# A mixture-of-experts drain of 34 slots instead of 36: five slots hold four experts of 32 tokens each

## The reference

```python
x = x + xattn(layernorm(x), ctx, ctx, Wq, bq, Wk, bk, Wv, bv, Wd, bd)
def ffn(h, w_red, wg, W1, b1, W2, b2):          # h: 4096 x 256, from layernorm(x)
    logits = (h @ w_red) @ (wg / norm(wg)).T    # 8 experts
    gates = softmax(logits); score = max(gates); idx = argmax(gates)
    u = gelu(h @ W1[idx] + b1[idx])             # 256 -> 512, own expert only
    return (u @ W2[idx] + b2[idx]) * score      # 512 -> 256
x = x + ffn(layernorm(x), ...)
```

## Time and profile before

| | |
|---|---|
| median of 3 runs | 344.08 us (343.32 to 344.24) |
| the profiled execution | 343.6 us |
| its span in the trace | 341.8 us |
| PE busy | 322.5 us, 94% of the span |
| DVE, POOL, ACT busy | 74%, 70%, 58% |
| TensorE clock granted | full in every slice |
| DMA | busy 0.9 and more until 190 us, then about 0.25 |

### The profile page before, as it was taken

How to read it: one execution, slowest core, us unless ns; L and a number is a source line. 1 busy time by engine, 2 the same in 40 slices (tenths; PEclk the granted TensorE clock), 3 DMA queues, 4 the chain that set the end, 5 groups by cost and what they waited for, 6 DMA issues and landing times.

```text
span 341.8 us, 10746 instructions
## 1 busy us (share of the span) xinstructions
PE 322.5 (94%) x3723; PEld 270.3 (79%) x3723; DVE 252.6 (74%) x718; ACT 199.7 (58%) x532; POOL 238.9 (70%) x379
## 2 busy tenths in 40 slices
PE   6999899999999999999788799989999999999995
PEld 5777678888888888777666688979898999996485
DVE  7545698888898888899887756885866666665563
ACT  1001577787778777867874745784567533443451
POOL 3598699999989999978888767552765545554323
PEclk9999999999999999999999999999999999999999
DMA  6699899999999999999999112240222222222100
GB/s 231 223 287 303 244 265 255 257 271 251 260 276 288 308 312 315 305 293 286 308 349 396 48 33 79 70 139 33 78 82 77 63 75 66 73 66 78 33 15 32
DMA packets 54838, 63.45 MB, mean 186 GB/s; under 512 B 36335, under 2 KB 45696, under 8 KB 54785
## 3 DMA queue, kind: packets, MB, share of 16 engines
q1 hardware_dynamic: 50544, 52.77, 52.7%
q0 software_dynamic: 3456, 9.12, 9.1%
q10 hardware_dynamic: 784, 0.87, 0.7%
HBM read 41.59 MB, written 21.68 MB: 185 GB/s over the span
## 4 chain that ended last, share of the span: by engine, by line
PE 77%; DVE 8%; issue 5%; ACT 4%; POOL 3%; DMA 2%; DVEq 1%; ACTq 0%; SPq 0%; POOLq 0%
PE bQ L1357 15%; PE bL L1307 7%; PE bKV L1118 7%; PE bY L1172 7%; PE bQ L1214 7%; PE bKV L1307 7%; PE bKV L1115 7%; PE bO L1138 5%; PE bL L1127 4%; PE bA L1226 3%; PE bT L1319 2%; DMA r<-in_xc 2%; PE bQ L1350 2%; PE bKV L1295 1%; PE bO L1273 1%
## 5 line engine op out<-in xcount | busy, mean ns | idle before, releaser
L1357 PE MATMUL bQ<-w,wA 128*128 x256 | 61.1, 381 | 1.5 <-issue 1.1
L418 POOL TENSOR_TENSOR x<-ql,mask 128x1024 f32<-128x1024 f32 x32 | 60.6, 1893 | 2.7 <-DVE r L748 0.5
L1000 ACT ACTIVATE pad<-ql 64x512 f32<-64x512 f32 x64 | 40.0, 625 | 22.2 <-DMA ql<-qkv_scr 21.8
L1357 PEld LDWEIGHTS bQ<-w,wA 128*128 128x128 f32 x256 | 46.2, 190 | 8.2 <-issue 3.2
L480 POOL DMA_INDIRECT out<-r,ids x23 | 23.2, 1010 | 41.3 <-DVE r L910 41.3
L500 POOL DMA_INDIRECT r<-row_scr,idg x36 | 37.2, 1033 | 14.7 <-issue 14.7
L1023 ACT ACTIVATE ax<-bA,mask 128x256 f32<-128x256 f32 x91 | 36.3, 473 | 3.5 <-PE bA L1226 3.3
L1172 PE MATMUL bY<-wD,oT 128*128 128x265 f32 x128 | 34.6, 392 | 1.4 <-ACT oT L988 1.3
L1078 ACT ACTIVATE wA<-bL,r 128x128 f32<-128x128 f32 x68 | 19.4, 373 | 25.3 <-PE bL L1307 25.3
L1214 PE MATMUL bQ<-wA,r 128*128 128x265 f32 x128 | 33.9, 387 | 0.3 <-DVE wA L536 0.3
L1115 PE MATMUL bKV<-wA,r 128*128 128x256 f32 x128 | 33.0, 380 | 1.1 <-DMA r<-in_xc 0.6
(11 more groups left out here) (213 smaller groups left out, 688.4 us busy)
## 6 DMA issues: line engine op xcount, KB each, us to landing
qkv_scr<-qkv SPq DMA_DIRECT2D x16, 768.0 KB, 4.7
ql<-qkv_scr SPq DMA_DIRECT2D x32, 384.0 KB, 5.8
r<-in_xc SPq DMA_DIRECT2D x15, 512.0 KB, 5.8
row_scr<-cat SPq DMA_DIRECT2D x32, 133.5 KB, 6.1
w1b<-in_W1b SPq DMA_DIRECT2D x8, 514.0 KB, 7.1
w<-in_W SPq DMA_DIRECT2D x8, 512.0 KB, 7.0
xt<-in_x SPq DMA_DIRECT2D x15, 256.0 KB, 5.9
b2b<-in_b SPq DMA_DIRECT2D x2, 512.0 KB, 6.8
```

The costliest lines, as they stand in the source:

```text
L418: eng.tensor_tensor(quarter(kx[:, z % 2, :]), spread(ql[z // 2 % 2][:, :, z % 2, 0:HD]), mask_k, ALU.mult).then_inc(S["kx"], 1)
L1000: i_ = eng.activation(pad[n, z % 3, :].rearrange("p (k g h d) -> p k g h d", k=2, g=NG_, h=2) [:, :, :, h, :], ql[z // 2 % 2][n, :, z % 2, ...
L1357: i_ = eng.matmul(down_bank(b)[:, 0:C], hT[b % 2][:, k, :], w2[:, bass.ds(eb * (KH * C) + k * C, C)], start=(k == 0), stop=(k == KH - 1))
```

## The change

- `NS` goes from 36 to 34. An expert's rest is put either into a whole slot or into quarters of 32 tokens; five slots hold four quarters each, of any four experts. They are no longer neighbours: `MIX_SLOTS` = (20, 23, 26, 29, 32). `S2` is 21.
- Which experts' rests get a whole slot goes by their size: `vector_late` ranks the eight rests (parts 1 to 3), and part 13 is shorter.
- A mixed slot's first and second product run as four tiles of 32 columns. The first expert's matrices are those in SBUF; the other three experts' are loaded again from DRAM by SP, in `sync_quarters` (six transfers of 512 KB for each mixed slot, in two sets of buffers that the attention stage leaves free; the third set waits for the first to be used).
- Both biases of a mixed slot are gathered by token from a new input `b12` (b1 and b2 of each expert in one row of 3 KB): `pool_bias`, one for each of steps 15 to 19. DVE adds the first as it copies the hidden values out; the gelu is one instruction over 512 columns instead of eight; the second bias takes one DVE instruction instead of two.
- `scalar_second` is gone.

The diff, cut:

```diff
-MIX = 3
-NS = NT + NE - 1 - MIX
+MIX = 5
+QUARTER = P // 4
+QUARTERS = P // QUARTER
+NS = ((NTOK + NE * (QUARTER - 1)) // QUARTER + QUARTERS - 1) // QUARTERS
...
-MIX_AT = NS - 3 - MIX
+MIX_STEP = 3
+MIX_SLOTS = tuple(NS - 2 - MIX_STEP * (MIX - 1 - j) for j in range(MIX))
...
+        def sync_quarters(eng, j):
+            if j == 0:
+                eng.wait_ge(S["texp"], 1)
+                eng.wait_ge(S["idg"], 1)
...
+            if j > 1:
+                eng.wait_ge(S["up"], MIX_SLOTS[j - 2] + 1)
+            e = [eng.value_load(texp[0:1, u:u + 1], min_val=0, max_val=NE - 1) for u in units(MIX_SLOTS[j])[1:]]
+            for h, e_h in enumerate(e):
+                eng.dma_start(first[j % 2][h], W1b.rearrange("e p n -> (e p) n")[bass.ds(e_h * P, P), 0:KC * HID]
+                              ).then_inc(S[f"first{j % 2}"], 16)
+            if j > 1:
+                eng.wait_ge(S["down"], MIX_SLOTS[j - 2] + 1)
+            for h, e_h in enumerate(e):
+                eng.dma_start(second[j % 2][h], W2.rearrange("e p n -> (e p) n")[bass.ds(e_h * P, P), :]
+                              ).then_inc(S[f"second{j % 2}"], 16)
...
+            if 0 <= s - BIAS_AT < MIX:
+                pool_bias(eng, s - BIAS_AT)
...
             if part == 2:
-                after(eng.scalar_tensor_tensor(odd, til, float(P), rest, ALU.mult, ALU.is_lt))
+                after(eng.scalar_tensor_tensor(key8, io_e[:, 0, :], 1.0 / 16, rem, ALU.mult, ALU.add))
+                after(eng.tensor_tensor(gt8, key8.unsqueeze(1).broadcast_to((P, NE, NE)),
+                                        key8.unsqueeze(2).broadcast_to((P, NE, NE)), ALU.is_gt))
+                eng.tensor_reduce(ftot, full_l, AX, ALU.add)
+                after(eng.tensor_reduce(rank, gt8, AX, ALU.add))
+                eng.tensor_scalar(q32, rem, (QUARTER - 1.0) / 2, ROUND_QUARTER, ALU.add, ALU.add)
+                after(eng.scalar_tensor_tensor(reach, rank, float(P), ftot.broadcast_to((P, NE)), ALU.mult, ALU.add))
+                eng.tensor_scalar(q32, q32, ROUND_QUARTER, None, ALU.subtract)
+                after(eng.tensor_scalar(w128, reach, float(WHOLE * P), float(P), ALU.is_lt, ALU.mult))
...
@@ vector_hidden
-                eng.tensor_copy(w1s[a % 2][:, 0:HID], bH[a % 2][:, :]).then_inc(S["hid"], 1)
+                eng.wait_ge(S[f"bias{j}"], 16)
+                eng.tensor_tensor(w1s[a % 2][:, 0:HID], bH[a % 2][:, :], bias[j][:, 0:HID],
+                                  ALU.add).then_inc(S["hid"], 1)
...
@@ tensor_up
-                        eng.matmul(bH[a % 2][0:HALF, :], gT[a % 2][:, c, 0:HALF],
+                        eng.matmul(bH[a % 2][0:QUARTER, :], gT[a % 2][:, c, 0:QUARTER],
                                    w1f[:, bass.ds(e0 * W1W + c * HID, HID)], start=(c == 0), stop=(c == KC - 1))
-                        i_ = eng.matmul(bH[a % 2][HALF:P, :], gT[a % 2][:, c, HALF:P],
-                                        second1[j][:, c * HID:(c + 1) * HID], start=(c == 0), stop=(c == KC - 1))
+                        for h in range(1, QUARTERS):
+                            i_ = eng.matmul(bH[a % 2][quarter_rows(h), :], gT[a % 2][:, c, quarter_rows(h)],
+                                            first[j % 2][h - 1][:, n], start=(c == 0), stop=(c == KC - 1))
```

More of the change, by code:

```diff
@@ L60 @@
 FILLS_ROWS = 8
-SECOND_AT = NEXT + 6
+BIAS_AT = NEXT + 7
 INVERSE_IN = (NEXT + 3, NEXT + 4)
@@ L97, in mixed, with quarter_rows, build @@
 def mixed(s):
-    return MIX_AT <= s < MIX_AT + MIX
+    return s in MIX_SLOTS
 def column(s):
-    return s if s < MIX_AT else s + NS - MIX_AT - MIX if mixed(s) else s - MIX
+    return NS - MIX + MIX_SLOTS.index(s) if mixed(s) else s - sum(1 for m in MIX_SLOTS if m < s)
 def units(s):
-    return [S1 + WHOLE + 2 * (s - MIX_AT) + h for h in range(2)] if mixed(s) else [column(s)]
-def build(nc, x, xc, wkvT, wqT, wdT, Wd, bkvq, bd, bd_col, w_redT, wgT_in, wg, W1b, W2, b2, out):
+    return [S1 + WHOLE + QUARTERS * MIX_SLOTS.index(s) + h for h in range(QUARTERS)]
+def quarter_rows(h):
+    return slice(QUARTER * h, QUARTER * (h + 1))
+def build(nc, x, xc, wkvT, wqT, wdT, Wd, bkvq, bd, bd_col, w_redT, wgT_in, wg, W1b, W2, b2, b12, out):
     f32, bf16, i32 = mybir.dt.float32, mybir.dt.bfloat16, mybir.dt.int32
@@ L203, in build @@
         ids = sb("ids", [P, NSP], i32)
-        texp = sb("texp", [P, S1 + UNITS], i32)
+        texp = sb("texp", [P, S1 + UNITS + MIX], i32)
         ohe = oh[:, :, :].rearrange("p n e -> p e n")
@@ L232, in build @@
         key, top, inc = late(0, NT - R1, NE), late(96, NT - R1), late(128, NE, NT)
-        rest, texc, shift, over, rank, delta, unit = (late(640 + 8 * k, NE) for k in range(7))
+        rest, texc, shift, full_l, rem, q32, key8, rank, reach, w128, uexc, delta = (late(384 + 8 * k, NE)
+                                                                                     for k in range(12))
+        ftot = late(480, 1)
+        gt8 = late(512, NE, NE)
         both, inc2 = late(2240, 2 * NE), late(2256, 2 * NE)
-        til, odd, tinc, oinc = both[:, 0:NE], both[:, NE:2 * NE], inc2[:, 0:NE], inc2[:, NE:2 * NE]
-        last8, far = late(2272, NE), late(2280, R1)
+        whole, part_q, tinc, uinc = both[:, 0:NE], both[:, NE:2 * NE], inc2[:, 0:NE], inc2[:, NE:2 * NE]
+        far = late(2280, R1)
         exc, slot, lim = late(704, NE, NT), late(960, NE, NT), late(1216, NE, NT)
@@ L252, in build @@
         bH = [bKV, bL]
-        second1 = [x0[:, W1W * j:W1W * (j + 1)] for j in range(MIX)]
-        first_bias = [x0[:, W1W * MIX + KH * j:W1W * MIX + KH * (j + 1)] for j in range(MIX)]
-        second2 = [fl(xt)[:, KH * C * j:KH * C * (j + 1)] for j in range(MIX)]
+        bias = [x1[:, (HID + C) * j:(HID + C) * (j + 1)] for j in range(MIX - 1)] + [sb("bias4", [P, HID + C])[:, :]]
+        B = KC * HID
+        taken_x0 = [x0[:, B * k:B * (k + 1)] for k in range(4)]
+        taken_xt = [fl(xt)[:, B * k:B * (k + 1)] for k in range(3)]
+        taken_q = [b[:, :, :, :].rearrange("p x t w -> p (x t w)")[:, 0:B] for b in (*qkv, *ql)]
+        first = [taken_xt, taken_x0[0:3]]
+        second = [[taken_x0[3], *taken_q[0:2]], [*taken_q[2:4], ax[:, :]]]
         def spread(in_):
@@ new lines, in vector_late @@
+                eng.tensor_scalar(q32, q32, ROUND_QUARTER, None, ALU.subtract)
+                after(eng.tensor_scalar(w128, reach, float(WHOLE * P), float(P), ALU.is_lt, ALU.mult))
+            if part == 3:
+                eng.tensor_tensor(whole, full_l, w128, ALU.add)
+                after(eng.scalar_tensor_tensor(part_q, w128, 0.0, q32, ALU.is_equal, ALU.mult))
+                after(eng.tensor_tensor_scan(inc2, one8[:, :], both, 0.0, ALU.mult, ALU.add))
+                after(eng.tensor_tensor(texc, tinc, whole, ALU.subtract))
+                eng.tensor_tensor(uexc, uinc, part_q, ALU.subtract)
+                after(eng.tensor_tensor(shift, texc, taken[:, :], ALU.subtract))
@@ L797, in vector_late @@
-                after(eng.tensor_scalar(delta, rank, -float(HALF), float(S2 * P), ALU.mult, ALU.add))
+                after(eng.tensor_tensor(lim, tinc.unsqueeze(2).broadcast_to((P, NE, NT)), slot, ALU.is_le))
             if part == 5:
@@ L862, in vector_weights @@
                 eng.wait_ge(S["texp"], 1)
-            if slotted(n):
-                held_v[n] = [eng.value_load(texp[0:1, u:u + 1], min_val=0, max_val=NE - 1) for u in units(n)]
-                if mixed(n) or n in TAKEN_BY_SCALAR:
+            if slotted(n) and not mixed(n):
+                ex = held_v[n] = eng.value_load(texp[0:1, column(n):column(n) + 1], min_val=0, max_val=NE - 1)
+                if n in TAKEN_BY_SCALAR:
                     return
-                ex = held_v[n][0]
                 if n > 1:
@@ L1369, in _ @@
             sync_attention(eng)
+            for j in range(MIX):
+                sync_quarters(eng, j)
         @engines.gpsimd
```

116 lines of the change are left out of this document (50 added, 66 removed).

## The result

The changed kernel takes **339.92 us** (median of six runs, 339.33 to 340.42); the kernel before, in six runs beside it, 343.92 (343.32 to 346.15). The ratio is 0.9877, with a 95% interval of 0.9853 to 0.9901: faster, by about 4 us, a small change but clear of the noise. The forecast was 340.2, in a range of 338.3 to 343.4. The profiled execution of the changed kernel took 339.95, where the sum had 339.7 and the one of before 343.6: 3.65 us less. Its span is 338.2 against 341.8.

A forecast was written before the change was run, and what follows sets the result against it. PE was taken to bound the drain, busy 59.75 of 60 us from 250 to 310 us. Terms -7.46 + 2.1 + 1.2 - 0.2 + 0.5 = -3.9 us gave a forecast of 340.2 us, range 338.3 to 343.4.

The forecast's parts named there:

- two slots fewer: 36 slots become 34: two plain steps of 3.73 us on PE go, -7.46 us, with nothing else under them.
- five mixed slots for three: Five separate mixed slots at 1.07 us above plain ones, against 3.25 for three in a row: +2.1 us.
- the routing on DVE: More small DVE instructions in steps 7 and 8 make PE wait in steps 8 and 9: +1.2 us.
- part 13, step 14: DVE's part 13 gets shorter, giving back some of PE's 0.42 us wait in step 14: -0.2 us.
- the matrices: SP's reloads from DRAM, 15.7 MB on a queue and engines a quarter busy, stay hidden: 0 us.
- ACT's copies gone: The copies that ACT no longer makes lay beside PE's work, so removing them gains 0 us.
- late gathers: Steps 15 to 19: bias gathers make POOL lag 2.8 us, cutting the row gathers' lead to 6.4: +0.5 us.
- the tail: The end after the last second product; no term of its own, nothing else taken to lie under the two removed steps.
- I take four: In mixed slots, four 32-column tiles run at a time on PE, 0.43 us per 512-column pass, rather than two at 0.86.
- fourth rival: Matrices not there in time, SP's transfers at half rate beside the gathers: some 6 us, 346; chance 0.07 with other losses.
- the nearest row: The trace row for late gathers: row gathers land in 3.0 us at the median, up to 6.9; 6.9 gave +0.5.
- first rival: Gathers come late, costing 2 to 4 us instead of 0.5, POOL's queue perhaps falling behind: 341.7 to 344; chance 0.18.

The follow-up runs named there:

- The experiment on the kernel before: Nine small instructions, six of them waited for, added to DVE's routing in the kernel before, nothing else of the change: 345.71 us against 343.83, ratio 1.0058.

## Why the prediction was right

| term | predicted us | what the traces show |
|---|---|---|
| two slots fewer | -7.46 | -7.46 |
| five mixed slots for three | +2.1 | +1.6 |
| the routing on DVE | +1.2 | +1.2 |
| part 13, step 14 | -0.2 | -0.05 |
| the matrices | 0 | 0 |
| ACT's copies gone | 0 | -0.7 |
| late gathers | +0.5 | +1.1 in steps 15 to 21 |
| step 27 | none | +0.3 |
| the tail | 0 | +0.4 |

The first, the third and the fifth term came in as worked out, and they carry most of the result. That the total was only 0.25 us off (339.95 against 339.7) is luck in part: six terms were each off by 0.2 to 0.7, with signs that cancelled.

**The mixed slots.** "I take four" was the step that decided the sign, and it holds: the passes are 0.43 and 0.22 apart. The price was a little too high. Of 1.07 us for a slot that stands alone, 0.99 was measured, and the difference is in the second product. In the steps 4.29, 3.96 and 3.93 long from 275.38 on, the first product and the transposes cost 0.56, as the prediction had from the earlier trace rows. The second product costs 0.23, where the prediction had 0.32. Its 0.32 was what a step of the old block had left after the gelu's wait was taken off, and that number was mis-sized. The five slots together cost 4.9 (no step stands behind the last one) against 3.25, +1.6.

**The routing.** All three steps came in as worked out. PE's second product of step 8 in the changed kernel, and its first product of step 9:

```profile
217.11 1.99 PE L1390 MATMUL bQ<-w,wA 128*128 x8 [0.19 <-DVE r L959]
...
219.67 2.02 PE L1336 MATMUL bL<-wA,r 128*128 128x128 f32 x16 [0.57 <-issue]
```

They stood at 216.72 and 218.45. The first is 0.39 us later (predicted 0.4), the second starts at 219.67 (predicted 219.6). DVE's last instruction of step 7 ends at 216.97 (predicted 216.9). The experiment on the kernel before shows that the instructions alone do this.

**Step 14, a step that failed.** The prediction read "PE waited 0.42 us for DVE" and gave 0.2 of them back. In the changed kernel the step takes 4.67 us for 4.72, so next to nothing came back:

```profile
245.38 0.44 PE L1348 MATMUL bT<-ident,r 128*128 128x128 f32 x2
...
246.22 1.99 PE L1390 MATMUL bQ<-w,wA 128*128 x8 [0.41 <-DVE r L959]
```

Part 13 did get shorter as worked out. DVE's result, the one that the profile names, came 2.43 us after the step's first product (245.81) instead of 2.70 (244.84), 0.27 earlier. But the product came no earlier than the rows let it: from the transposes to it are 0.84 us here and 0.85 before (244.18 to 245.03), while most steps have 0.22. The wait was put down to what had its semaphore last, but what ended last was PE's own register load behind late rows, 0.90 us after ACT's scaling in this kernel. With the load moved, the step was 0.26 us shorter; there the product starts 0.15 us after DVE's result (246.22), so only then does part 13 count.

**The matrices.** Hidden, as forecast: SP begins at 246.64 instead of the 244 that I had worked out, the window runs at 400 GB/s, and PE waits for none. Three apart they have more than the 11 us that I gave them: the third set for a first product is issued at 279.33 and wanted at 300.02. Two apart was enough as well. One apart, a slot's matrices are wanted with each step of some 4.6 us and take 8, and the kernel took 11 us more than the changed one. The fourth rival was right that sets in series turn the change to a loss when their cover is gone; its half rate beside the gathers did not come, and the distance of the slots alone keeps the loss away. The Trainium skill (DMA: Bandwidth & Descriptors, "Specifications") has some 358 GB/s as a core's limit; the window from 250 us shows 400 for 15 us, with one core at work, so the trace disagrees again.

**The late gathers and ACT's copies.** The step from the change to late rows was right; the step from late rows to PE was not, and one term was put at nothing that was not nothing. Waits of ACT for the gathered rows (start, length, engine, what; in brackets the wait) in steps 18 and 21 (step 20 is shown above):

```profile
259.75 0.60 ACT L1083 ACTIVATE r<-r 128x256 f32<-128x256 f32 x1 [1.11 <-DMA r<-row_scr,idg]
...
271.96 0.60 ACT L1083 ACTIVATE r<-r 128x256 f32<-128x256 f32 x1 [1.96 <-DMA r<-row_scr,idg]
```

The row gathers issued from 248 to 270 us land after 6.3 to 7.0 us; the source view answers the earlier trace rows with 2.8, 4.4 and 7.2. The 6.9 of the nearest row was the typical value of that stretch. POOL's lag came out larger than worked out: the gather of slot 19's rows starts 5.8 us ahead of step 20 (261.05) instead of 9.5, a lag of 3.7 where the prediction had 2.8. ACT took the rows as they landed, 6.9 us later. But the prediction counted the lead to ACT's first use at 265.94, and PE's transposes came 1.5 us after ACT was done there (268.02). That slack took up the lateness: the transposes of steps 18, 20 and 21 start where they do in plain steps. The steps lost 1.13 us together (1.22 over plain steps, less the 0.09 of the step ahead of a mixed slot), because PE's register load stands behind the wait for the rows; the experiment with the load moved shows it. That is a step of the prediction that failed: it had PE late by a wait for rows, and had no term for the load.

The other is "The copies that ACT no longer makes lay beside PE's work: 0 as well". The kernel before had lost 0.73 us in steps 17 and 19 by the same load, behind rows that ACT scaled late between its copies; with the copies gone that loss is gone. The balance of the two is +0.40, near the predicted 0.5 by luck.

Step 27 takes 4.20 us for 3.93 in the changed kernel's profile, with 0.20 us of "issue". In every other profile of a kernel with these mixed slots it takes 3.92 or 3.93, also where the bias gathers stand as they did, so it may belong to this one execution. Its cause stays open.

By the rule of the first rival (the Trainium skill, DMA: Bandwidth & Descriptors, "Queues, rings and completion order") a DMA engine changes queues only at a packet's end, and the prediction made of it that POOL's queue would fall behind. Landings of 6.3, 7.0, 6.5, 6.9 and 6.6 us in turn, while some 400 GB/s flow, show a delay of 3 to 4 us that doesn't grow.

**The tail.** From the last second product to the end 0.41 us more, 0.3 of it in the last scatter. The kernel before without its last two slots has 0.39 of it too, and nothing else of the change, so it isn't a price of the quarters or of the new transfers. In both the last slot stands right behind a mixed one; whether that is the reason was not tried.

## What to carry to other kernels

When a step that is limited by one engine holds a register load behind a wait, look at the distance from the end of that wait to the instruction behind the load, and not only at the releaser that the profile names. A lag of a queue and a late landing can each be free and cost an engine a stall together, so spread the extra transfers over the steps in which they are wanted. Transfers that are hidden three steps apart can turn a change into a loss one step apart, so work out from bytes and rate how often a set can come. And when work is taken away beside the bounding engine, look for long steps near it before you put its worth at nothing.

## What the runs showed of the hardware

- A register load from on-chip memory costs about 0.6 us on PE when it can't run ahead (0.84 us from transposes to product instead of 0.22), and the product behind it starts 0.90 to 0.96 us after the rows that it stands behind are ready. On DVE the gaps with such a load behind a routing part were 0.82 and 0.95 us.
- Four float32 tiles of 128 by 32 run at the same time. At the full clock a pass of 512 columns takes 0.43 us for all four and one of 256 takes 0.22.
- Row gathers that land in 3.0 us at the median take 6.3 to 7.0 beside bulk loads at 400 GB/s. The bias gathers land in 6.6 to 7.6.
- In the version with adjacent mixed slots the granted clock was 0.50 (the 1.2 GHz level) for PE's work just behind a wait of 4.04 us for a matrix, and 1.00 (2.4 GHz) again some 4 us later; it cost 1.6 us. In the changed kernel it is 1.00 in all windows shown.
